# A graph network's edge stage: the gathered rows are added by identity matmuls instead of by VectorE

## What is computed

```
messages = gelu(edge_input @ mW1 + mb1) @ mW2 + mb2
gates    = sigmoid(gelu(edge_input @ gW1 + gb1) @ gW2 + gb2)
aggregated = segment_sum(messages * gates, dst)
```

## Time and profile before

| | |
|---|---|
| median of three runs | 10923.42 us |
| span of the profiled execution | 10933.0 us |
| edge stage, from the first to the last segment sum | 161.7 to 5789.8 us |
| busy over the span: PE, DVE, ACT, POOL | 75%, 45%, 25%, 59% |
| 1000 to 5000 us, busy: PE, DVE, ACT, POOL | 3034, 2510, 1767, 2232 us of 4000 |
| 1000 to 5000 us, mean granted TensorE clock | 0.86 of 2.4 GHz |

### The profile page before, as it was taken

The page is one execution under the profiler, slowest core; times in us unless marked ns, Lnnn a source line. Parts: engine busy times, 40 slices in busy tenths (PEclk is TensorE's granted clock), DMA queues, the critical chain, the costliest instruction groups (busy, mean ns, idle before and its releaser), DMA issues. The chain is left out here.

```text
span 10933.0 us, 150076 instructions
## 1 busy us (share of the span) xinstructions
PE 8192.3 (75%) x42144; PEld 5220.9 (48%) x42144; DVE 4899.6 (45%) x11836; ACT 2690.1 (25%) x6600; POOL 6435.5 (59%) x6424
## 2 busy tenths in 40 slices
PE   4777777777777777777777578887777577887776
PEld 4555555555555555555555233333334333433333
DVE  7666666666666666666667122222222121222222
ACT  3444444444444444444443000000000000000000
POOL 4555555555555555555554666666664666666663
PEclk7888888888888888888887788888887688888887
DMA  4444444444444444444444456666565465666656
GB/s 147 123 138 131 136 132 136 132 135 132 135 133 135 133 135 135 134 135 133 135 132 134 155 207 220 216 218 214 208 212 198 156 215 206 224 217 210 210 207 207
DMA packets 933049, 1818.03 MB, mean 166 GB/s; under 512 B 277359, under 2 KB 745600, under 8 KB 875312
## 3 DMA queue, kind: packets, MB, share of 16 engines
q10 hardware_dynamic: 65600, 773.65, 18.6%
q1 hardware_dynamic: 615456, 578.39, 16.9%
q0 software_dynamic: 251856, 464.10, 14.8%
HBM read 1361.12 MB, written 454.48 MB: 166 GB/s over the span
## 5 line engine op out<-in xcount | busy, mean ns | idle before, releaser
L962 POOL DMA_INDIRECT hid<-src_table,src_ids x3127 | 3136.7, 1003 | 2510.4 <-ACT msg L1358 1590.2
L1240 PE MATMUL bd<-ring,table_sb 128*96 128x480 f32 x6272 | 2941.6, 614 | 513.3 <-issue 511.7
L1240 PEld LDWEIGHTS bd<-ring,table_sb 128*96 128x96 f32 x6272 | 1071.7, 176 | 2131.6 <-issue 2131.1
L1007 POOL DMA_INDIRECT hid<-conv_table,hid x1596 | 1561.9, 979 | 751.1 <-issue 486.2
L1155 PE MATMUL sg<-hot,msg 128*98 128x64 f32 x6272 | 831.1, 286 | 1115.9 <-ACT msg L1358 1105.2
L1132 PE MATMUL bd<-one_hot_dst,one_hot_src 128*128 128x168 bf16 (+1 forms) x10368 | 1277.0, 274 | 253.5 <-issue 252.3
L1007 POOL DMA_INDIRECT feat_in<-conv_table,hid x1056 | 1026.1, 972 | 545.2 <-issue 324.6
L1155 PEld LDWEIGHTS sg<-hot,msg 128*98 128x98 f32 x6272 | 746.8, 199 | 1252.2 <-issue 1180.0
L1972 DVE TENSOR_TENSOR acc<-acc,sg 96x64 f32 x400 | 87.2, 218 | 2450.0 <-remote 1652.7
L1132 PEld LDWEIGHTS bd<-one_hot_dst,one_hot_src 128*128 128x128 bf16 x10368 | 1007.1, 110 | 299.1 <-issue 284.3
L1367 ACT ACTIVATE blocks<-bd 128x480 f32<-128x480 f32 (+1 forms) x1152 | 658.1, 571 | 1704.7 <-PE bd L1132 811.8
(11 more groups left out here) (248 smaller groups left out, 10307.8 us busy)
## 6 DMA issues: line engine op xcount, KB each, us to landing
ring<-adjacency ACTq DMA_DIRECT2D x448, 1680.0 KB
adjacency<-blocks SPq DMA_DIRECT2D x384, 980.0 KB
attr<-in_attr SPq DMA_DIRECT2D x392, 128.0 KB
hid<-src_table,src_ids POOLq DMA_INDIRECT x3127
hid<-conv_table,hid POOLq DMA_INDIRECT x1596
feat_in<-conv_table,hid POOLq DMA_INDIRECT x1056
conv_table<-table_sb SPq DMA_DIRECT2D x28, 336.0 KB, 2.4
feat_half<-feat_keep SPq DMA_DIRECT2D x56, 168.0 KB
```

The lines of the kernel that those rows point to most:

```text
L962: pool.indirect_dma_start(out=hid[s][:, t, :], out_offset=None, in_=src_rows, in_offset=bass.IndirectOffsetOnAxis(ap=src_ids[h][:, j:j + 1 ...
L1007: pool.indirect_dma_start(out=conv_g[j][slot][:, t, :], out_offset=None, in_=conv_rows[l], in_offset=bass.IndirectOffsetOnAxis(ap=conv_ids ...
L1240: op = nc.tensor.matmul(side_ps[w].rearrange("r (o z) -> r o z", o=UNIT_OCTETS), table_sb[:, D * k:D * (k + 1)], ring[slot][:, :, OCTET_FA ...
```

## The change

TensorE no longer only makes the attribute product: `add_rows` multiplies the gathered rows with a 128 x 128 identity and accumulates them in the same two banks. It waits for the quad's gathers, and it, not VectorE, now signals `s_added`. Gelu reads the sum from PSUM and writes `hid[s]`. A bank pair is free again when gelu has read it (`s_gelu`). VectorE's `add` is gone.

```diff
                 if free:
-                    pe.wait_ge(s_added, QUADS_PER_ITER * n + s - 1)
+                    pe.wait_ge(s_gelu, QUADS_PER_ITER * n + s - 1)
                 for h in range(2):
                     last = nc.tensor.matmul(
                         attr_ps[s % 2][:, 512 * h:512 * h + 2 * H2], attr[s // 2][:, P * (s % 2):P * (s % 2 + 1)],
-                        w_attr[:, 2 * H2 * h:2 * H2 * (h + 1)], start=True, stop=True)
+                        w_attr[:, 2 * H2 * h:2 * H2 * (h + 1)], start=True, stop=False)
                 last.then_inc(s_attr_mm, 1)
+
+            def add_rows(it, n, s):
+
+                pe.wait_ge(s_gath[s], gathered(it, QUAD, QUAD_SPARED[s]))
+                flat = hid[s][:, :, :].rearrange("p t f -> p (t f)")
+                for h in range(2):
+                    last = nc.tensor.matmul(attr_ps[s % 2][:, 512 * h:512 * h + 2 * H2], ident[:, :],
+                                            flat[:, 2 * H2 * h:2 * H2 * (h + 1)], start=False, stop=True)
+                last.then_inc(s_added, 1)
...
                     if build:
                         build_part(2 * s, nb, places)
+                    if s + 2 < QUADS_PER_ITER:
+                        add_rows(it, n, s + 2)
+                    elif not last:
+                        add_rows(it + 1, n + 1, s + 2 - QUADS_PER_ITER)
                     pe.wait_ge(s_gated, QUADS_PER_ITER * n + s + 1)
...
             def gelu(n, s):
                 act.wait_ge(s_added, QUADS_PER_ITER * n + s + 1)
-                flat = hid[s][:, :, :].rearrange("p t f -> p (t f)")
-                nc.scalar.activation(flat, flat, ACT.Gelu).then_inc(s_gelu, 1)
+                nc.scalar.activation(hid[s][:, :, :].rearrange("p (b t) f -> p b (t f)", b=2),
+                                     attr_ps[s % 2][:, :].rearrange("p (b c) -> p b c", b=2)[:, :, 0:2 * H2],
+                                     ACT.Gelu).then_inc(s_gelu, 1)
...
-            def add(it, n, s):
-
-                i = QUADS_PER_ITER * n + s
-                dve.wait_ge(s_gath[s], gathered(it, QUAD, QUAD_SPARED[s]))
-                dve.wait_ge(s_attr_mm, i + 1)
-                pair = hid[s][:, :, :].rearrange("p (b t) f -> p b (t f)", b=2)
-                v.tensor_tensor(pair, attr_ps[s % 2][:, :].rearrange("p (b c) -> p b c", b=2)[:, :, 0:2 * H2], pair,
-                                ALU.add).then_inc(s_added, 1)
```

More of the change, by code:

```diff
@@ L1141, in edges @@
                 if first:
-                    for s in range(3):
-                        attr_product(n, s, s == 2)
+                    for s in range(2):
+                        attr_product(n, s, False)
+                        add_rows(it, n, s)
+                    attr_product(n, 2, True)
                 for s in range(QUADS_PER_ITER):
@@ L1718, in edges @@
                 if first:
-                    add(it, n, 0)
-                    add(it, n, 1)
                     dot(n, 0, True)
@@ L1737, in edges @@
                         dot(n + 1, 0, False)
[L1738 to L1741, removed]
                 if last:
```

## The result

The kernel after took 11,054.8 us (median of 4 runs, 11,037.9 to 11,065.9), the kernel before 10,923.5 us: a ratio of 1.0116, with a 95% interval of 1.0101 to 1.0130. It is slower, by 131 us. The forecast was slower by 722 us: the sign is right, and the size is 5.5 times too large. Which terms of the sum were wrong is the matter of what follows.

A forecast was written before the change was run, and what follows sets the result against it. Bound: a ring of POOL's gathers, PE's late signals and ACT's weighing, 14.20 us per pair of quads. After: 10.03 + 1.72 + 3.29 + 1.0 = 16.04, +1.84 x 392 = +721 us, giving 11,645 us; range 11,050 to 12,300.

The forecast's parts named there:

- the sign: Whole kernel: the change makes it slower, chance 0.81, against faster 0.15 and same 0.04.
- The bound: Edge stage, per pair of quads: eight gathers, PE's late signal, ACT's copy and weighing, POOL's restart sum to 14.20 us.
- DVE's adds worth 0: VectorE in the edge stage: removing its adds, 743 us in all, takes 0 off the path.
- PE's work hidden: PE in the edge stage: identity matmuls, 2.6 to 5.2 us per pair, may just fit in 2.3 to 4.6 free.
- the term of 1.0 us: PE's half-clock spells, formerly hidden, fall in step (2)'s chain: 1.0 us per pair, bounds 0 and 2.7.
- Step (1): ACT after PE's late signal: gelu now precedes copy and weighing, 3.29 us in place of 2.45 until POOL goes on.
- Step (2): PE's queue: attribute product waits for gelu, delaying the block part; weighed 8.2 us after release, POOL's fifth gather at 8.3.
- Step (3): PE waits for a quad's gathers ahead of other matmuls: counted 0, bound 1.7 us once per pair.
- The likeliest case: Edge stage: 16.04 us per pair against 14.20, +721 us, 11,645 us in all; chance 0.45.
- only the gelu is added: Edge stage: clock stays up or low spells fall into idle time; +0.84 us per pair, +329 us, 11,250; chance 0.20.

The follow-up runs named there:

- the run with the small add: Kernel before, with VectorE's add cut from 768 to 16 columns: 10,950.7 us, 0.9993.
- the bank freed by gelu: Kernel before, with VectorE's add writing back into PSUM, gelu reading it there, and the attribute product waiting for gelu: 10,988.1 us, 1.0032.
- the drained run of the kernel before: Kernel before, with GpSimd waiting after each quad's four gathers until they have landed: 11,938.7 us, 1.0914.
- drained gathers in the kernel after: Kernel after, with GpSimd waiting after each quad's four gathers until they have landed: 11,777.7 us, 1.0766.

## Why the prediction was right, and where it was wrong

- **The bound: right.** POOL's bursts, PE's late signal, copy, weighing. The cycle of eight of the kernel after has the same sum: 10.24 + 1.59 + 0.48 + 1.16 + 0.81 = 14.28 us from 3020.88, against 14.20. Leaving out half of the gathers gave 17.7%. Why PE's signals are late stays open.
- **DVE's adds worth 0: right,** by the run with the small add.
- **PE's work hidden: right, short of 0.2%.** Doubled attribute products cost 0.19%, and cutting the identity products gave nothing clear back (1.0101 against 1.0116, intervals overlap). The clock I took the wrong way round: the term of 1.0 us rests on time at 1.2 GHz, and on the mean this fell, with the granted clock at 0.93 and 0.86 before.
- **Step (1), gelu in the chain, +0.84 us in every cycle: this step failed.** It put gelu's signal together with the block part's, let through at the same moment. In the cycle of eight shown, gelu's came 3 us earlier (3029.67 against 3032.71), and gelu fitted between, as in 127 of 167 such cycles. Measured: +0.13 us per cycle of eight. The added work alone gives as much (14.39 us), but so does the change with that work cut (14.41), so whose it is stays open. With the attribute product moved, gelu's place costs at most 0.08 us per pair, a tenth of the forecast.
- **Step (2), the attribute product waits for gelu, "just in time at the full clock": the mechanism was right, its price misjudged.** I gave it 0 at the full clock and 1.0 us per pair as a term for half-clock spells, in all pairs. It strikes in 30% of the quads, where it breaks the burst of eight, and costs 0.6 us in each: 0.28 us per pair on the mean (2 x 0.14), in place of the 1.84 that (1) and (2) made together. The move of the attribute product takes back 0.9 points of the 1.16%, in the kernel after alone: this is shown. "Just in time at the full clock" was too tight even so: with the late gelu the same steps, from gelu at 3005.21 to the end of the weighing at 3013.74, took 8.5 us at the full clock, where the forecast had 8.2, and the fifth gather at 8.3.
- **Step (3), no wait for gathers: right** (5.2 and 0.5 us before the identity products of the two banks).
- **What the forecast said would be seen:** gelu, copy, weighing in a row: in 37 of 167 cycles of eight. Bursts of four: yes, as foretold. PE over 80%: 84%. A pair of 15 to 17 us: 14.73 on the mean (5776 / 392), 15.54 only where both quads stand in cycles of four. DVE -740 us: -620. Convolutions within 20 us: 15.
- **What is left** after the move, 0.28%, agrees with the price of PE's work (0.19%), of the bank freed by gelu (0.32%), or of gelu's place ahead of the weighing; these runs can't tell them apart.

The likeliest case added a full price to every cycle where the chain has slack in most. The rival "only the gelu is added" (11,250) was nearer, by luck: its 0.84 us per cycle isn't what was lost.

## What to carry to other kernels

Ask of an engine's in-order queue what stands behind an instruction that gets a new wait: here the wait cost 0.9% only because the segment sum and block part that ACT wanted were queued behind it, and moving the waiting instruction to the end of the turn took that back. Work added inside a wait of the same engine cost next to nothing here, as long as its own signal came before the one that ended the wait, so price it by when each signal comes and not by its duration. Freeing an engine that nobody waits for (DVE, 63% busy) gave 0.

## What the runs showed of the hardware that was not expected

- With more work on PE its granted clock was higher: 0.86 before, 0.96 with the attribute product made twice, 0.93 in the kernel after, 0.86 with the small add. Part of the added matmuls was paid by faster ones: in the kernel after, PE's busy time grew by 345 us in 4000 where 541 quads at 1.32 us are 714.
- With four indirect gathers issued one every 1.25 us, an engine that waited for them all went on 1.8 us (median; 4.9 or more in one of twenty) after the last was issued, and GpSimd itself, which waited too, 0.85 us later (the drained run of the kernel before).
- PE's signals arrive up to 6.7 us after the recorded ends of its matmuls while gathers stream, in half of the quads; with half of the gathers in 4 of 550, and with drained gathers in the kernel after in none of 352. The cause wasn't found.
